# A router and mixture of experts on one core: one payload row for both experts, results in neighbouring rows, and eight extra matmuls per step

## What is computed

```
h = layer_norm(x);  q, k, v = h @ Wq, h @ Wk, h @ Wv          (4 heads of 32)
x = x + softmax(causal(q k^T / sqrt(128))) v @ Wo + bo
nx = layer_norm(x)
noisy = nx @ Wr + br + noise * softplus(nx @ Wn + bn)         (8 experts)
router = softmax over the two highest of noisy
skip   = sigmoid(nx @ Wsk + bsk) > 0.5
out = x + sum_e router_e * (relu(nx @ W1_e + b1_e) @ W2_e + b2_e),  or x where skip
```

## Time and profile before

| | |
|---|---|
| median of 3 runs | 811.3 us (807.3 to 813.56) |
| the profiled execution | 814.46 us, its span 812.5 us |
| mean granted TensorE clock | 0.865 of 2.4 GHz |
| PE, DVE, ACT, POOL busy | 579.6, 576.5, 486.9, 413.0 us |
| steps | to about 480 us |
| experts | 480 to 703 us |
| last stage | 725 us to the end |

### The profile page before, as it was taken

The page is one execution under the profiler, slowest core; times in us unless marked ns, Lnnn a source line. Parts: engine busy times, 40 slices in busy tenths (PEclk is TensorE's granted clock), DMA queues, the critical chain, the costliest instruction groups (busy, mean ns, idle before and its releaser), DMA issues.

```text
span 812.5 us, 31537 instructions
## 1 busy us (share of the span) xinstructions
PE 579.6 (71%) x11012; PEld 455.5 (56%) x11012; DVE 576.5 (71%) x2270; ACT 486.9 (60%) x979; POOL 413.0 (51%) x478
## 2 busy tenths in 40 slices
PE   0466989989998998998865209999999999700000
PEld 0245767767776776777645207777777777500000
DVE  3366767887878788787664626777777777537887
ACT  2447666877877788687654208888888888400000
POOL 3000656677766777666655741666666666430000
PEclk9989989999999999999976559999999999855555
DMA  9764222332332332235443257777776777159997
GB/s 95 233 193 122 62 84 76 96 101 59 98 96 59 98 98 85 75 100 112 121 142 96 97 186 258 235 230 235 234 237 235 238 234 238 49 143 292 301 301 223
DMA packets 164172, 127.32 MB, mean 157 GB/s; under 512 B 38050, under 2 KB 142595, under 8 KB 164128
## 3 DMA queue, kind: packets, MB, share of 16 engines
q1 hardware_dynamic: 127264, 90.00, 37.8%
q10 hardware_dynamic: 24576, 20.98, 8.6%
q0 software_dynamic: 12288, 15.77, 6.1%
HBM read 73.86 MB, written 62.78 MB: 168 GB/s over the span
## 4 chain that ended last, share of the span: by engine, by line
PE 41%; DVE 22%; issue 14%; DMA 7%; ACT 5%; POOL 4%; DVEq 3%; ACTq 2%; SPq 1%; POOLq 0%
PE ps L547 6%; PE ps L504 6%; DMA out<-z 5%; DVE stats L830 4%; PE ps L569 4%; POOL expert_rows L1135 3%; PE ps L637 3%; PE ps L585 3%; PE ps L638 3%; PE ps L639 3%; PE ps L625 3%; PE ps L627 3%; PE ps L626 3%; DVE sc_m L873 2%; DVE smax L870 2%
## 5 line engine op out<-in xcount | busy, mean ns | idle before, releaser
L1135 POOL DMA_INDIRECT expert_rows<-pay,rows_of x256 | 254.2, 993 | 195.0 <-DVE rows_of L929 116.1
L1147 POOL DMA_INDIRECT expert_results<-z,words x128 | 135.1, 1055 | 106.9 <-DVE z L1028 75.6
L675 ACT ACTIVATE z<-xres,shift,rstd 128x128 f32 (+1 forms) x256 | 105.1, 483 | 34.4 <-DVE shift L864 34.4
L1042 DVE TENSOR_TENSOR hlo<-h,hhi 128x512 fp32r<-128x512 f32 x128 | 89.7, 701 | 45.7 <-ACT hhi L788 43.6
L786 ACT ACTIVATE h<-ps,w1x 128x512 f32<-128x512 f32 x128 | 88.3, 690 | 34.8 <-PE ps L627 31.3
L788 ACT ACTIVATE hhi<-ps,w1x 128x512 fp32r<-128x512 f32 x128 | 87.3, 682 | 0.0
L547 PEld LDWEIGHTS ps<-pT,v_sb 32*32 32x32 f32 x4096 | 48.4, 106 | 66.0 <-issue 64.6
L547 PE MATMUL ps<-pT,v_sb 32*32 32x32 f32 x4096 | 58.0, 204 | 35.7 <-DVE sc_m L873 25.2
L504 PE MATMUL ps<-ident,z 128*128 128x128 f32 x256 | 46.3, 310 | 25.8 <-ACT z L675 20.0
L637 PE MATMUL ps<-hhi,w2x 128*128 128x512 f32 x128 | 57.3, 447 | 4.2 <-issue 4.2
L527 PE MATMUL ps<-kT,qT 32*32 32x32 f32 x4096 | 55.8, 201 | 3.9
(11 more groups left out here) (147 smaller groups left out, 1321.5 us busy)
## 6 DMA issues: line engine op xcount, KB each, us to landing
w1x<-split_weights SPq DMA_DIRECT2D x33, 514.0 KB, 3.7
w2x<-split_weights SPq DMA_DIRECT2D x33, 512.5 KB
expert_results<-zeros SPq DMA_DIRECT2D x32, 512.0 KB
pay<-expert_rows SPq DMA_DIRECT2D x33, 264.0 KB, 3.6
xres<-in_r_x SPq DMA_DIRECT2D x32, 256.0 KB
split_weights<-w2x ACTq DMA_DIRECT2D x16, 512.0 KB
hhi<-expert_results SPq DMA_DIRECT2D x32, 256.0 KB, 3.7
hlo<-expert_results SPq DMA_DIRECT2D x32, 256.0 KB, 3.8
```

Source lines behind the costliest of these rows:

```text
L675: m = nc.scalar.activation(z[:, j:j + 1], tile(xres, n, j), ACT.Identity, bias=shift[:, which, j:j + 1], scale=rstd[:, which, j:j + 1])
L1042: ev.tensor_tensor(hlo[:, c], h32[:, c % 2], hhi[:, c].bitcast(F32), ALU.subtract).then_inc(s_h_lo, 1)
L1135: g.indirect_dma_start(rows, bass.IndirectOffsetOnAxis(ap=rows_of[:, odd, k * J + j:k * J + j + 1], axis=0), pay[:, odd, k, j, :], None, b ...
L1147: g.indirect_dma_start(results, bass.IndirectOffsetOnAxis(ap=words[:, slot, j:j + 1], axis=0), yrow[slot][:, j, :], None, bounds_check=K * ...
```

## The change

It does five things. The payload has one row per token for both experts, four buffers instead of two, and the second norm writes it in place (the copy L754 is gone). Its extra columns are the word (2 x token, copied from a table `words_all` by ScalarE) and the two experts' numbers, written by VectorE, which uses them for its one-hot tensor too. In the experts' stage `keep_words` adds 1 to the word where the block's expert isn't the first of the two. The two results of a token are therefore neighbouring rows of `expert_results`, and the last stage reads them with one DMA per group; it has four output buffers. With four payload buffers `pipeline` has four steps in its loop body. And TensorE does eight matmuls of a constant `filler`, 256 columns wide, into an unused part of a PSUM bank before each step's scores.

```diff
@@ names and buffers @@
-    results_t = results.rearrange("(k n p) c -> p k n c", k=K, p=P)
+    results_t = results.rearrange("(n p k) c -> p n k c", k=K, p=P)
+        filler = sb("filler", [P, 2 * P], BF16)
-        rows_of = sb("rows_of", [P, 2, K * J], U32)
-        token = sb("token", [P, K, J])
-        pay = sb("pay", [P, 2, K, J, RW])
+        rows_of = sb("rows_of", [P, 4, K * J], U32)
+        words_all = sb("words_all", [P, N // P])
+        pay = sb("pay", [P, 4, J, RW])
-        half = z1
-        fin = z2
+        fin = [z1[:, 0], z1[:, 1], z2[:, 0], z2[:, 1]]
...
@@ pipeline @@
             for t in range(-2, 5):
-                step(t, t % 2)
-            with eng.Fori(5, NG - 4, 2) as t:
-                step(t, 1)
-                step(t + 1, 0)
+                step(t, t % 4)
+            with eng.Fori(5, NG - 6, 4) as t:
+                for d in range(4):
+                    step(t + d, (5 + d) % 4)
...
@@ TensorE @@
+            def keep_clock(times):
+                for _ in range(times):
+                    nc.tensor.matmul(ps[:, 0, 2 * P:4 * P], ones[:], filler[:], start=True, stop=True)
...
                     apart(pe, (s_k_copied, n + 1),
                               (s_oT_made, n - 1),
                               (s_s_less, n))
+                    keep_clock(8)
                     for h in range(H):
...
-                    transposes(ps[:, 6, :], z2[:, par], s_z2T_made)
+                    transposes(ps[:, 6, :], pay[:, (turn + 2) % 4, :, 0:C], s_z2T_made)
...
@@ ScalarE @@
                     act.wait_ge(s_norm, (t + 3) * NORM)
-                    wait(act, s_z2T_made, n - 1)
-                    norm_rows(z2[:, par], 1, n).then_inc(s_z2, 1)
+                    slot = (turn + 2) % 4
+                    wait(act, sent[slot], quad(n, slot, SENT))
+                    nc.scalar.activation(pay[:, slot, :, C], words_all[:, bass.ds(n * J, J)], ACT.Copy)
+                    norm_rows(pay[:, slot, :, 0:C], 1, n).then_inc(s_z2, 1)
...
-                n = t - 2
-                if live(n):
-                    wait(act, sent[par], pair(n, par, SENT))
-                    nc.scalar.activation(pay[:, par, :, :, 0:C], z2[:, par].unsqueeze(1).to_broadcast([P, K, J, C]),
-                                         ACT.Copy).then_inc(s_pay_made, 1)
...
@@ VectorE @@
-                    ev.scalar_tensor_tensor(top_f[:], top_i[:, :, 0:K].rearrange("p j k -> p k j"), 1.0,
-                                            keep[:, bass.ds(n * J, J)].unsqueeze(1).to_broadcast([P, K, J]),
+                    slot = (turn + 1) % 4
+                    wait(dve, sent[slot], quad(n, slot, SENT))
+                    experts_of = pay[:, slot, :, C + 1:C + 1 + K]
+                    ev.scalar_tensor_tensor(experts_of, top_i[:, :, 0:K], 1.0,
+                                            keep[:, bass.ds(n * J, J)].unsqueeze(2).to_broadcast([P, J, K]),
                                             ALU.add, ALU.mult).then_inc(s_route, 1)
...
-                    wait(dve, sent[odd], pair(n, odd, SENT))
...
-                ev.tensor_copy(words[:, slot], xg[slot][:, :, C].bitcast(U32)).then_inc(s_words_kept, 1)
+                ev.scalar_tensor_tensor(words[:, slot], xg[slot][:, :, C + 1], exp_no[:, bass.ds(i, 1)],
+                                        xg[slot][:, :, C], ALU.not_equal, ALU.add).then_inc(s_words_kept, 1)
...
-                dve.wait_ge(f_in[slot], quad(n, slot, 16 * K) + 16 * K)
+                dve.wait_ge(f_in[slot], quad(n, slot, 16) + 16)
+                wait(dve, f_out[slot], quad(n, slot, 16))
...
-                wait(dve, f_out[par], pair(n, par, 16))
...
@@ SyncE @@
-                for k in range(K):
-                    sp.dma_start(yin[slot][:, k], results_t[:, k, bass.ds(n * J, J), :]).then_inc(f_in[slot], 16)
+                sp.dma_start(yin[slot], results_t[:, bass.ds(n * J, J), :, :]).then_inc(f_in[slot], 16)
...
@@ GpSimd @@
-                    apart(pool, (sent[odd], pair(n, odd, SENT)),
-                                (s_token_next, n + 1))
-                    g.tensor_copy(pay_u[:, odd, :, :, C], token[:]).then_inc(s_word_made, 1)
-                    apart(pool, (s_word_made, n + 1))
-                    g.tensor_scalar(token[:], token[:], float(G), None, ALU.add).then_inc(s_token_next, 1)
+                    slot = (turn + 1) % 4
                     apart(pool, (s_route, n * ROUTE + ROUTE),
-                                (s_pay_made, n + 1))
+                                (s_z2, n + 1))
                     for k in range(K):
                         for j in range(J):
...
-                                pay[:, odd, k, j, :], None, bounds_check=E * ER - 1,
+                                pay[:, slot, j, :], None, bounds_check=E * ER - 1,
```

## The result

The changed kernel takes **858.3 us** (median of 4 runs, 857.1 to 865.0) against 809.5 of the kernel before beside it (807.3 to 813.6): ratio 1.061, 95% interval 1.054 to 1.069. It is 49 us slower. The forecast was 831 with a range up to 848. The sign was right, and so was the main cause, code that is fetched again in each pass; but the eight matmuls, forecast as a gain of 6.8 us, cost some 18.

A forecast was written before the change was run, and what follows sets the result against it. The stage of steps, with closely matched ScalarE and TensorE chains, was taken as the bound; -6.8 + 28.9 + 7.5 - 2.6 - 2.2 - 5 + 0.2 = +20.0 on 811.3 gave 831 us, range 792 to 848 (own range 812 to 850).

The forecast's parts named there:

- the memset: GpSimd's memset of the filler, before the first step: +0.2 us.
- the 22 steps: Loop stretch from seventh to 29th group of v products, 265.3 us before; forecast +29.6 us.
- What bounds the kernel: Stage of steps: ScalarE and TensorE chains of nearly the same length, 12.06 us a step, 82 KB body kept without fetching.
- rival 1: Loop of steps: the longer body is kept, no fetch; -16.4 us, 795 in all; chance 0.27.
- rival 2: Loop of steps: code is fetched, but mostly behind the work; -3 us, 808 in all; chance 0.15.
- rival 3: Loop of steps: body kept, but the matmuls leave the seven clock falls; -5 us, 806; chance 0.06.
- The price of fetching, 28.9 + 7.5 = 36.4: TensorE's four-step body: 168 KB fetched each pass, +28.9 us over 22 steps; five jumps back, +7.5.
- Clock falls taken away: Loop of steps: eight matmuls fill TensorE's wait and end its clock falls; 11.75 us a step, -6.8 us.
- -2.6: Three late steps that also split weights: ScalarE's copy of the payload (L754) goes, -2.6 us.
- -2.2: GpSimd behind 432 us: without cast and addition, gaps between issue groups fall from 1.1 to about 0.35 us; -2.2.
- The last stage, -5: Last stage: 1 KB read pieces and four output slots save 0.16 us per tile, -5 us; ends 0 and -9.

The follow-up runs named there:

- experiment 1: The kernel before with a step-loop body of four steps instead of two on every engine, nothing else changed: 856.8 us against 810.1, ratio 1.056.
- experiment 4: The changed kernel without the eight matmuls, TensorE's body still four steps: 840.7 us, ratio 1.038 to the kernel before; its profiled execution took 830.4 us.
- experiment 2: The kernel before with the four-step body on TensorE alone, two steps on the other engines: 860.3 us, ratio 1.062 to the kernel before.
- experiment 3: The changed kernel with TensorE's loop code at two steps a pass, other engines at four: 819.9 us, ratio 1.011 to the kernel before.
- experiment 5: The kernel before with the eight matmuls in front of the mask matmuls and nothing else: 815.5 us, ratio 1.007 to the kernel before.
- experiment 9: The kernel before with four output buffers in the last stage, result rows still apart: 803.0 us against 812.8, ratio 0.985.
- experiment 6: The changed kernel with TensorE at two steps a pass and without the eight matmuls: 814.0 us, ratio 1.003 to the kernel before.
- experiment 7: The changed kernel without the eight matmuls, TensorE and VectorE both at two steps a pass: 798.1 us, ratio 0.983 to the kernel before.
- experiment 11: The kernel before with 300 tiny matmuls added to TensorE's two-step body, about 120 KB: 22 steps took 397.2 us; no total time given.
- experiment 12: The kernel before with 500 tiny matmuls added to TensorE's two-step body, about 144 KB: 22 steps took 460.6 us; no total time given.
- experiment 10: The changed kernel with TensorE and VectorE at two steps a pass, the eight matmuls only in the loop's steps: 794.1 us against 812.8, ratio 0.979.
- experiment 8: The kernel before with a token's two result rows side by side, read in one DMA, still two output buffers: 825.0 us, ratio 1.019.

## Why the prediction was right and wrong

By the medians, the long body alone cost 46.7 us (experiment 1) where the forecast had 36.4; the payload and the last stage then gave back 16.1 (experiment 4 against 1) where it had 9.6 with the memset; and the eight matmuls on top cost 17.6 where it had a gain of 6.8. So 24.4 of the missing 28 us are the eight matmuls.

In the two profiled executions the span grew by 43.7 us: 6.6 up to the first of the 22 steps, 54.3 in them, -8.1 from there to the first sum of the last stage (395.17 to 725.5 before, 456.09 to 778.3 after), -9.1 in the sums (82.4 to 73.3). The forecast had +29.6 for the 22 steps.

- **What bounds the kernel, and that the body is fetched again**: right. No packet in 265 us for 82 KB, 54 for 168 KB. Rivals 1 and 2 fall with the packets and experiments 1 to 3, and rival 3, which needs a body that is kept, with them.
- **The price of fetching, 28.9 + 7.5 = 36.4**: the mechanism was right and the size 7 too small. The long body alone costs 43.2 in the 22 steps (308.5 against 265.3). The factors that the prediction gives for its 28.9 make 28.6 to 29.5; that changes nothing.
- **"Clock falls taken away", -6.8**: this is the step that failed. In a loop whose code is kept it held (experiment 5: the clock at 1.00, 6.6 us less in the 22 steps, though a gain of that size is within chance). But I added it to a loop that, by my own next term, stops several times in each pass. There the clock falls behind the stops as well (0.92 over the 22 steps, not 1.00), and "issue" stops take the place of the waits that the eight matmuls fill: 319.6 us with them and 303.3 without, so +16.3 in place of -6.8. These 23.1 us, with the 6.8 above and the payload's -5.2 below, are the 24.7 that were missing in the 22 steps. By the caution in experiment 4 the +16.3 may be up to 10 too large; it would still be a loss, and the medians, which do not hang on that execution, have 17.6 in all.
- **The unrolled steps ahead of the loop**: I had priced the eight matmuls only in the loop. All of the steps before it are fetched as they are run, which the earlier trace rows showed. The changed kernel reaches the 22 steps 11.9 us later than without them (136.47 against 124.56), experiment 3 14.5 later and experiment 5 5.4.
- **The payload**: -7.0 up to the first of the 22 steps and -5.2 in them (experiment 4 against 1), where I had put +0.2 for the memset and nothing more. With the low profiled execution of experiment 4 both can be chance; the medians leave 7 us for the payload in all (840.7 against 856.8, of which the last stage is 9). Behind the loop -2.6 and -2.2 were forecast, and the stretch up to the last stage is 8.1 shorter. GpSimd's eight issues follow each other at 1.27 us with 0.30 between groups too, as forecast (0.35). This part was not run by itself.
- **The last stage, -5**: 9 gained, the far end of its range. But my reason was wrong, so the hit is luck: the larger pieces, which I had priced, give nothing, and alone they lose 17 in the stage. The waits for out, which I had let pay "only as far as the engines have room", are the whole gain. I had read the DMA share of 0.99 as engines that are full. In experiment 9 it is 1.12 over 735 to 790 us, so it counts some time twice, and 18.3 against 20.7 bytes per ns of that time is no safe measure of how fast pieces of 512 bytes move: with four buffers they moved 335 GB/s, and pieces of 1 KB 332.
- **Not seen at all**: VectorE's body. It hardly shows in the changed kernel (one wait of 3.0 us between 125 and 390), since TensorE's stops cover it, but it is the next 16 us as soon as they go (experiments 6 and 7).

## What to carry to other kernels

Before a loop body is made longer, count each engine's instructions in it: a body that is no longer kept is fetched whole in every pass, here 2 us a step. The busy shares do not name it; the packets on the instruction queue and the "issue" stops at the same places of each pass do. If a buffer's number needs four turns, keep the code at two and put the one instruction that differs behind a branch. Don't add up two edits when one takes away the ground of the other: work that fills a wait is worth something only where the wait, not the code, is what stops the engine.

## What the runs showed of the hardware

- TensorE went round a body of 82 KB with no instruction packet in 265 us; bodies of 120, 144 and 168 KB were fetched whole in each pass, 8.9, 10.0 and 11.8 packets of 16 KB (experiments 11 and 12, and the changed kernel). VectorE's long body came in 8 KB packets, with a stop of 2.5 us once a pass (experiment 3).
- A branch within a kept body costs TensorE little: with it a step takes 11.84 us, against 11.76 without (experiments 10 and 5). The two kernels differ in the payload too, and two executions of one kernel can differ by 0.3 a step.
- Filling a short wait with matmuls held the granted clock at 1.00 over 265 us where it had been 0.95 and fallen seven times (experiment 5).
- One 512 KB read in place of two of 256 KB made a write of 256 KB beside it land in 5.1 us instead of 3.6 (experiment 8), with four buffers 6.0 instead of 4.3.
- With four output buffers the last stage moved 335 GB/s with reads in pieces of 512 bytes and 332 with pieces of 1 KB (experiment 9 and the changed kernel, 55 us each); VectorE set the pace in both.
